# A Mamba-2 layer with a LoRA-expert branch on one Trainium2 core: VectorE turns every chunk's y, and B together with x, in the paired groups

## The reference

```python
xn = layernorm(x)                                  # x: 2048 tokens x 1024
proj = xn @ in_proj_w.T                            # gate 4096 | x 4096 | B 1024 | C 1024 | dt 64
x, B, C = split(silu(causal_conv4(proj_hbc)))      # 64 heads of 64; 8 groups, B and C 128 wide each
dt = softplus(dt + dt_bias); dA = exp(-exp(A_log) * dt)
state_t = state_{t-1} * dA_t + (dt_t * x_t) outer B_t ;  y_t = state_t @ C_t + x_t * D
yn = rmsnorm_by_group(y) * norm_weight * silu(gate)
out = x_in + yn @ out_proj_w.T + (xn @ W_base.T + b_base + top-2 LoRA experts)
```

## Time and profile before

| what | value |
|---|---|
| median of 3 runs | 3145.19 us (3144.51 to 3145.26) |
| the profiled execution, its own time | 3145.09 us |
| its span, first to last instruction | 3143.4 us |
| PE busy | 3126.1 us, 99% |
| DVE busy | 2558.5 us, 81% |
| ACT busy | 1704.5 us, 54% |
| POOL busy | 835.5 us, 27% |
| granted TensorE clock | 1.00 of full speed throughout |

### The profile page before, as it was taken

One profiled execution on the slowest core, in us unless ns is written; L12 is line 12 of the kernel. 1 busy time (PEld: TensorE's weight loads), 2 busy tenths in 40 slices (PEclk: granted clock), 3 DMA queues, 4 the chain that ended last, 5 costly groups with the idle time before them and its releaser, 6 DMA issues.

```text
span 3143.4 us, 55218 instructions
## 1 busy us (share of the span) xinstructions
PE 3126.1 (99%) x17660; PEld 2573.4 (82%) x17660; DVE 2558.5 (81%) x4599; ACT 1704.5 (54%) x4467; POOL 835.5 (27%) x917
## 2 busy tenths in 40 slices
PE   8999999999999999999999999999999999999999
PEld 7788888887888888888788888888878888888887
DVE  7977777785589999999648999999954988989983
ACT  5766666664265555656226555556533655565551
POOL 4444434433022222222103222222210222222220
PEclk9999999999999999999999999999999999999999
DMA  8777777777665555555566555555546555555554
GB/s 290 274 265 272 264 276 266 261 256 263 232 216 194 189 201 187 189 194 201 173 225 205 191 191 191 201 184 190 209 166 236 196 195 187 195 194 201 186 189 161
DMA packets 185668, 672.63 MB, mean 214 GB/s; under 512 B 21056, under 2 KB 22208, under 8 KB 185408
## 3 DMA queue, kind: packets, MB, share of 16 engines
q1 hardware_dynamic: 161280, 584.91, 53.3%
q10 hardware_dynamic: 24128, 84.42, 7.6%
...
## 4 chain that ended last, share of the span: by engine, by line
PE 95%; DVE 2%; ACT 1%; DMA 1%; issue 0%; SPq 0%; POOL 0%; ACTq 0%; DVEq 0%; POOLq 0%
PE dense L1072 21%; PE dense L1074 21%; PE dense L1073 21%; PE pX L1072 7%; PE pX L1074 7%; PE pX L1073 6%; PE pY L1187 3%; PE pD L1217 1%; PE pD L1187 1%; DVE conv_us L1497 1%; PE pCB L1163 1%; PE pU L1072 1%; PE pS L1073 1%; PE pS L1072 1%; PE pS L1074 1%; PE pU L1074 1%
## 5 line engine op out<-in xcount | busy, mean ns | idle before, releaser
L1072 PE MATMUL dense<-xn_hi,w_hl 128*128 128x512 f32 (+2 forms) x2192 | 869.7, 397 | 0.8 <-POOL w_hl L444 0.5
L1074 PE MATMUL dense<-xn_hi,w_hl 128*128 128x512 f32 (+2 forms) x2192 | 853.7, 389 | 0.0
L1073 PE MATMUL dense<-xn_lo,w_hl 128*128 128x512 f32 (+2 forms) x2192 | 852.0, 389 | 0.0
L1497 DVE SCALAR_TENSOR_TENSOR conv_us<-conv_in,const_g,conv_us 128x512 f32<-128x512 f32 x576 | 480.3, 834 | 47.0 <-ACT conv_us L694 33.2
L1074 PEld LDWEIGHTS dense<-xn_hi,w_hl 128*128 128x128 f32 (+1 forms) x2192 | 409.5, 187 | 88.9
L1072 PEld LDWEIGHTS dense<-xn_hi,w_hl 128*128 128x128 f32 (+1 forms) x2192 | 409.9, 187 | 86.0 <-issue 2.2
L1073 PEld LDWEIGHTS dense<-xn_lo,w_hl 128*128 128x128 f32 (+1 forms) x2192 | 410.3, 187 | 83.5 <-issue 1.2
L1072 PE MATMUL dense<-z_hi,w_hl 128*128 128x512 f32 x820 | 324.4, 396 | 1.6 <-DVE acc L1680 1.1
L501 POOL TENSOR_TENSOR C_lo<-BC,C_hi 128x128 fp32r<-128x128 f32 x120 | 60.0, 500 | 983.5 <-ACT S_hi L736 982.9
L1074 PE MATMUL dense<-z_hi,w_hl 128*128 128x512 f32 x820 | 319.7, 390 | 0.0
L1073 PE MATMUL dense<-z_lo,w_hl 128*128 128x512 f32 x820 | 319.1, 389 | 0.0
...
## 6 DMA issues: line engine op xcount, KB each, us to landing
...
cum_b<-cum_scratch ACTq DMA_DIRECT2D x128, 512.0 KB, 4.9
...
```

Source lines behind the costliest of these rows:

```text
L1072: nc.tensor.matmul(out, lhs[0], rhs[0], start=start, stop=False)
L1073: nc.tensor.matmul(out, lhs[0], rhs[1], start=False, stop=False)
L1074: return nc.tensor.matmul(out, lhs[1], rhs[0], start=False, stop=stop)
L1497: nc.vector.scalar_tensor_tensor(out=conv_u[r], in0=conv_in[r][:, t:t + TB], scalar=const_g[p][:, 4 * j + t:4 * j + t + 1], in1=conv_u[r], ...
```

## The change

All of it is in the paired groups (and what they call). It puts x and B into one tensor xBC, and `x_rows` turns x and B of two chunks together, as 16 transposes of 32x320 (5 tiles x 2 chunks x 32 tokens); `B_rows` goes. `yn_rows`, `gated_pair` and `gated_lo_pair` take chunks 2 and 3 as well, so `chunk_3` stays in a paired group for group 0's chunk 3 alone. On TensorE `chunk_1(0)` moves behind gate unit 2, and `chunk_2s(0)` and `chunk_2b(0)` behind out unit 0. ScalarE's `chunk_1` is split into `b_high`, `cs_high`, `ramps`, `wx_high` and `next_cum`, VectorE's into `wx_product`, `dtx_product`, `b_low` and `cb_masked`, and these are put into a new order. On VectorE x unit 2 goes ahead of y of chunks 2 and 3, x unit 3 behind it; turning y is spread between taps of tiles 4 and 5; silu of tile 3 comes ahead of tile 4's taps; silu of tile 5, the low part of z and `prep` move into the next group, behind the first quarter of `x_rows`. `chunk_2y` also waits for both products with dt.

```diff
 xn_lo = sb("xn_lo", [128, KD, TB], F32R)
 w_raw = [sb(f"w_raw{i}", [128, 1024]) for i in range(2)]
 w_hl = [sb(f"w_hl{i}", [128, 2, 2, 512], F32R) for i in range(2)]
-xT = [sb(f"xT{i}", [128, XT, TB]) for i in range(2)]
-BC = [sb(f"BC{i}", [128, 2, TB]) for i in range(2)]
+xBC = [sb(f"xBC{i}", [128, XT + 2, TB]) for i in range(2)]
+xT = [t[:, 0:XT, :] for t in xBC]
+BC = [t[:, XT:XT + 2, :] for t in xBC]
 BT, CT = ([bc[:, i, :] for bc in BC] for i in range(2))
 gate = sb("gate", [128, XT, TB])
 conv_us = sb("conv_us", [128, 2, TB])
...
-x_tm = sb("x_tm", [128, 2, GC])
-B_tm = sb("B_tm", [128, NC, N])
+x_tm = sb("x_tm", [128, 2, GC + N])
...
+    if not second:
+        normalize(0, 3)
     gate_unit(1)
-    chunk_1(g, p, 0, last, two=True)
-    z_high(g - 1, 3)
+    cs_high(g, p, 0)
+    if not second:
+        b_high(g, 0, True)
+        wx_high(g, 0)
+        z_high(0, 3)
+    gate_unit(2)
+    ramps(g, 0, True)
+    next_cum(g, 0, last)
+    gate_unit(3)
+    if second:
+        b_high(g, 0, True)
+        wx_high(g, 0)
     skip(g, 0)
-    gate_unit(2)
-    gate_unit(3)
     skip(g, 1)
-    chunk_1(g, p, 1, last, two=True)
+    b_high(g, 1, True)
+    wx_high(g, 1)
+    cs_high(g, p, 1)
+    ramps(g, 1, True)
+    next_cum(g, 1, last)
     if last:
         router_copy()
     mean_square(g, 0, True)
     mean_square(g, 1, True)
-    def normalize_pair():
-        normalize(g, 0, True)
-        normalize(g, 1, True)
-    chunk_1(g, p, 2, last, two=True, behind_wx=normalize_pair)
+    b_high(g, 2, True)
+    cs_high(g, p, 2)
+    wx_high(g, 2)
+    normalize(g, 0, True)
+    normalize(g, 1, True)
+    ramps(g, 2, True)
+    next_cum(g, 2, last)
     skip(g, 2)
     if not last:
         x_unit(0)
         ev_conv(g, K_X + 1, 1, turn_bank(12 + 1), p)
         tanh_conv(g, 0)
-    chunk_1(g, p, 3, last, two=True)
+    b_high(g, 3, True)
+    cs_high(g, p, 3)
+    wx_high(g, 3)
+    ramps(g, 3, True)
+    next_cum(g, 3, last)
     skip(g, 3)
-    z_high_pair(g, p)
+    z_high_pair(g, p, 0)
     if not last:
         x_unit(2)
         x_unit(3)
-        x_unit(4)
     mean_square(g, 2, True)
     mean_square(g, 3, True)
+    normalize(g, 2, True)
+    normalize(g, 3, True)
     if last:
-        normalize(7, 2, True)
-        normalize(7, 3, True)
-        z_high(7, 2)
-        z_high(7, 3)
+        z_high_pair(7, 1, 2)
     else:
-        normalize(g, 2, True)
-        x_unit(5)
-        z_high(g, 2)
+        x_unit(4)
+        ev_conv(g, K_X + 5, 5, turn_bank(12 + 5), p)
+        tanh_conv(g, 4)
+        z_high_pair(g, p, 2)
         tanh_conv(g, 5)
...
     gate_unit(g, False, 0, True)
-    if second:
-        chunk_3(g - 1, 2, two=True)
     gate_unit(g, False, 1, True)
+    gate_unit(g, False, 2, True)
+    if not second:
+        chunk_3(0, 3)
     chunk_1(g, 0, p, True, True)
-    gate_unit(g, False, 2, True)
-    chunk_3(g - 1, 3, two=second)
     gate_unit(g, False, 3, True)
+    out_units(g, 0, two=True)
     chunk_2s(g, 0)
     chunk_2b(g, 0)
-    out_units(g, 0, two=True)
+    out_units(g, 1, two=True)
     chunk_1(g, 1, p, True, True)
-    out_units(g, 1, two=True)
     if last:
         router_transpose()
     out_units(g, 2, two=True)
     chunk_2b(g, 3)
     chunk_2y(g, 2, True)
     chunk_2y(g, 3, True)
-    x_units(2)
-    if last:
-        chunk_3(7, 2, two=True)
-        x_units(1)
-        chunk_3(7, 3, two=True)
-        x_units(1)
+    x_units(4 if last else 2)
 group(0, 0, first=True)
...
     if first == 0:
-        dve.wait_ge(post, post_n(q, g, XT - 1))
+        dve.wait_ge(post, post_n(q, g, XT))
         dve.wait_ge(xd_done, chunk(q, g, c) + 1)
         dve.wait_ge(xw_done, chunk(q, g, c) * 2)
+        dve.wait_ge(ck_evac, chunk(q, g, c))
+        dve.wait_ge(bl_done, chunk(q, g, c))
     for f in range(first, end):
         for k in range(4):
-            src = xT[p][32 * f:32 * f + 32, :, :].rearrange("n j (c t) -> n j c t", c=NC)
-            dst = x_tm[32 * k:32 * k + 32, :, :].rearrange("p c (j i) -> p j c i", j=XT)
+            src = xBC[p][32 * f:32 * f + 32, 0:XT + 1, :].rearrange("n j (c t) -> n j c t", c=NC)
+            dst = x_tm[32 * k:32 * k + 32, :, :].rearrange("p c (j i) -> p j c i", j=XT + 1)
             ins = nc.vector.transpose(dst[:, :, :, 32 * f:32 * f + 32], src[:, :, c:c + 2, 32 * k:32 * k + 32])
     if end == 4:
         ins.then_inc(xt_done, 1)
-def B_rows(g, p, first, end):
-    if first == 0:
-        dve.wait_ge(post, post_n(q, g, XT))
-        dve.wait_ge(ck_evac, chunk(q, g, 0))
-        dve.wait_ge(bl_done, chunk(q, g, 0))
-    for f in range(first, end):
-        for k in range(4):
-            src = BT[p][32 * f:32 * f + 32, :].rearrange("n (c t) -> n c t", c=NC)[:, :, 32 * k:32 * k + 32]
-            ins = nc.vector.transpose(B_tm[32 * k:32 * k + 32, :, 32 * f:32 * f + 32], src)
...
+def wx_product(g, c):
+    if last_block and c == NC - 1:
+        return
+    if c == 0:
+        dve.wait_ge(prep_done, q * PREPS + g + 2)
+    dve.wait_ge(xt_done, xt_n(q, g, c))
+    nc.vector.tensor_tensor(heads(wx[:]), heads(x_tm[:, c % 2, 0:GC]), per_head(1, c), ALU.mult).then_inc(xw_done, 1)
+def dtx_product(g, c):
+    dve.wait_ge(xt_done, xt_n(q, g, c))
+    nc.vector.tensor_tensor(heads(dtx_2[c % 2]), heads(x_tm[:, c % 2, 0:GC]), per_head(0, c), ALU.mult)\
+        .then_inc(xw_done, 2 if last_block and c == NC - 1 else 1)
+def b_low(g, c):
+    dve.wait_ge(ck_evac, chunk(q, g, c) + 1)
+    nc.vector.tensor_tensor(B_lo[:], x_tm[:, c % 2, GC:GC + N], B_hi[:].bitcast(F32), ALU.subtract)\
+        .then_inc(bl_done, 1)
+def cb_masked(g, c):
+    dve.wait_ge(s1, chunk(q, g, c) * 2 + 2)
+    nc.vector.tensor_tensor(CBm, pCB[:, N:N + Q], causal[:], ALU.mult).then_inc(cbm_done, 1)
...
+def gated_pair(g, p, c):
+    cs = slice(c * Q, (c + 2) * Q)
     dve.wait_ge(gate_done, grp(q, g) * XT + XT)
-    dve.wait_ge(yt_done, (q - 1) * (G - 1) + g)
-    z = xT[p][:, :, 0:2 * Q]
-    nc.vector.tensor_tensor(z, z, gate[:, :, 0:2 * Q], ALU.mult).then_inc(z_done, 2)
...
             silu(g, 5, 1 - p)
-        if not first_block:
-            B_rows(g + 1, 1 - p, 0, 4)
         prep(g + 1)
...
     j_first = 1 if last else 0
-    x_rows(g, 0, p, 1 if second else 0, 4)
-    chunk_1_x(g, 0, True)
-    gated(g - 1, 3)
-    chunk_1_cb(g, 0, True)
-    gated_lo(g - 1, 3)
-    gate_tile(g, 0, False)
-    gate_tile(g, 1, False)
+    x_rows(g, 0, p, 0, 1)
+    if second:
+        silu(g - 1, 5, p)
+        gated_lo_pair(g - 1, 1 - p, 2)
+        prep(g)
+        x_rows(g, 0, p, 1, 2)
+        gate_tile(g, 0, False)
+        gate_tile(g, 1, False)
+        x_rows(g, 0, p, 2, 4)
+        wx_product(g, 0)
+        dtx_product(g, 0)
+        gate_tile(g, 2, False)
+        b_low(g, 0)
+    else:
+        x_rows(g, 0, p, 1, 4)
+        wx_product(g, 0)
+        gated(0, 3)
+        b_low(g, 0)
+        gated_lo(0, 3)
+        gate_tile(g, 0, False)
+        gate_tile(g, 1, False)
+        dtx_product(g, 0)
+        gate_tile(g, 2, False)
+    cb_masked(g, 0)
     masked(g, 0, True)
-    gate_tile(g, 2, False)
+    gate_tile(g, 3, False)
+    dve.wait_ge(acc_loaded, (q + 1) * 64)
+    out_adds(g, 0, halves=(0,), two=True)
     if last:
         router_weights()
+    out_adds(g, 0, halves=(1,), two=True)
     y_state(g, 0, True)
     y_skip(g, 0, True)
-    gate_tile(g, 3, False)
     state(g, 0)
-    dve.wait_ge(acc_loaded, (q + 1) * 64)
-    chunk_1_x(g, 1, True)
-    out_adds(g, 0, halves=(0,), two=True)
+    wx_product(g, 1)
+    dtx_product(g, 1)
+    b_low(g, 1)
     x_rows(g, 2, p, 0, 1)
-    out_adds(g, 0, halves=(1,), two=True)
-    x_rows(g, 2, p, 1, 2)
     if not last:
         consts_next(g, p)
     out_adds(g, 1, halves=(0,), two=True)
-    chunk_1_cb(g, 1, True)
+    x_rows(g, 2, p, 1, 2)
+    cb_masked(g, 1)
+    out_adds(g, 1, halves=(1,), two=True)
     x_rows(g, 2, p, 2, 3)
-    out_adds(g, 1, halves=(1,), two=True)
     masked(g, 1, True)
+    out_adds(g, 2, halves=(0,), two=True)
     x_rows(g, 2, p, 3, 4)
-    out_adds(g, 2, halves=(0,), two=True)
+    out_adds(g, 2, halves=(1,), two=True)
     y_state(g, 1, True)
-    out_adds(g, 2, halves=(1,), two=True)
     y_skip(g, 1, True)
     state(g, 1)
     y_intra(g, 0, True)
     y_intra(g, 1, True)
-    chunk_1_x(g, 2, True)
-    chunk_1_cb(g, 2, True)
+    wx_product(g, 2)
+    b_low(g, 2)
+    dtx_product(g, 2)
+    cb_masked(g, 2)
     out_adds(g, 3, halves=(0,), two=True)
-    yn_rows(g, p, 0, 1)
+    yn_rows(g, p, 0, 0, 1)
     out_adds(g, 3, halves=(1,), two=True)
-    yn_rows(g, p, 1, 3)
+    yn_rows(g, p, 0, 1, 3)
     if last:
         x_unit(0)
-    yn_rows(g, p, 3, 4)
+    yn_rows(g, p, 0, 3, 4)
     masked(g, 2, True)
     if last:
         x_unit(1)
     y_state(g, 2, True)
     y_skip(g, 2, True)
     state(g, 2)
-    gated_pair(g, p)
+    gated_pair(g, p, 0)
     if not last:
         x_unit(0)
-    chunk_1_x(g, 3, True)
+    wx_product(g, 3)
+    dtx_product(g, 3)
     x_unit(j_first + 1)
-    chunk_1_cb(g, 3, True)
```

(83 more changed lines are left out.)

109 lines of the change are left out of this document (68 added, 41 removed).

## The result

The changed kernel takes 3203.12 us (median of 4 runs, 3201.49 to 3204.52) against 3145.23 us (4 runs, 3144.51 to 3146.12): a ratio of 1.0184, 95% interval 1.0166 to 1.0201. The direction was forecast, the size was not: +58 us where the prediction had +19, and 3203 lies above the top of its range, 3182. The profiled execution took 3203.78, its span 3202.0.

What follows compares the result with a forecast made beforehand. TensorE was taken as the bound, VectorE nearly level; after the change VectorE would bound at 89.6 us a group against 87.1. At +6.4 a block, +19 in all, 3145.09 becomes 3164 us; whole range 3131 to 3182.

Steps and rivals of the forecast that it cites:

- TensorE's saving: On TensorE, each chunk_3 removed saves 0.48 us; 42 go in blocks 1 to 3, 20.2 us; a steady group needs 87.1.
- VectorE's sum: VectorE's need per steady group after the change: 87.5 + 7.1 - 5.0 + 2.2 - 0.1 - 3.3 + 1.2 = 89.6 us.
- the forecast distance: VectorE's x_tm transposes, grown from 256 to 320 columns, take about 0.51 us from start to start; +2.2 a group.
- The new wait: VectorE waits for normalised y before turning the second pair, behind x unit 3: +1.2 us a group, ends 0 and 1.7.
- The 1.55: VectorE's wait for conv_us before the taps of tile 3 goes, part of the -3.3 us a group.
- the waits of 1.27 that were to stay: VectorE's waits for the first pair's z_hi and y stay; 0 to -1.3 more if ScalarE's order removes one.
- The hold-up of gate tiles 0 and 1: Gate tiles wait for GpSimd's low part of S (1.29): VectorE needs 90.9, time 3184; rival with chance 0.10, left out of sum.
- B_lo of chunk 1: On VectorE before the change, it runs 0.80 for 0.28 while GpSimd makes wx_lo; with its end, taken as 0.6 us slack.
- the prediction's own formula: Per block, TensorE waits 5 x (89.6 - 87.1) + 0.6 = 13.1 and saves 14 x 0.48 = 6.7: +6.4 us.
- The prediction's "never" for a single SBUF input: VectorE instructions with one SBUF input are never locked out by GpSimd; those with two wait a whole instruction.
- the same meeting: TensorE's y product of chunk 3 meets VectorE's mask with 1.15 slack; 0.6 late in group 1, nothing added in group 7.
- The 0.6 of slack itself: Before the change VectorE by itself needs 88.07 - 0.6 = 87.5 us a group, against TensorE's 88.07.

Runs made afterwards that it cites:

- section 3: 15 of 16 transposes of the second pair's y left out: changed kernel 3153.16 us; two ScalarE moves added 3152.45; on section 4's 3135.38 us kernel 3124.88, 87.10 a group.
- r11_turn_late: Section 4's 3135.38 us kernel with the last 8 transposes of the first pair's y behind chunk 3's products, low z behind its mask: 3124.93 us.
- r2_gates: Changed kernel with ScalarE's high parts of C and S of chunk 0 moved behind gate unit 2 in groups 2 to 7: 3167.01 us, 89.6 a group.
- section 6: Rows of the kernel before; then the first pair's last 8 y transposes moved where GpSimd works, in reordered changed kernels: 3134.14, 3163.23 and 3124.93 us.
- sections 5 and 4: 5: kernel before with two wait-removing moves, 3144.97 us. 4: r2_gates with three such moves, 3135.38; also with high B and wx ahead of gate unit 3, 3155.32.

## Why the prediction was right and wrong

**TensorE's saving** was right: 0.48 for each of 42 `chunk_3`, 87.1 a group, shown by section 3 and, with all of the work done, by `r11_turn_late`.

**VectorE's sum** was right in its main terms. Four transposes of 32x320 take 2.05, 0.51 each; the forecast distance was 0.512. The new wait is 1.20 for 1.2. The 1.55 is gone. Smaller misses cancel: the waits of 1.27 that were to stay are 0.99 (z_hi) and 0.78 (yn), and a wait of 0.40 for B_hi has come. Without the two hold-ups the group is 89.6 (`r2_gates`), the very sum of the prediction, which to the tenth is luck, and 3167 is the forecast 3164 and 3 us.

**The step that failed** is "My sum leaves it out, since the two must coincide within a microsecond; its lower end is nothing." The hold-up of gate tiles 0 and 1 was costed, at most 1.3, and set aside with a chance of 0.10; it came in the steady groups, 1.0 each (all of them last the same 91.7 in blocks 1 and 2), under the decay of S right behind the low part that I had looked at. Coincidence was the wrong picture: what meets in one group meets in all 18, and GpSimd's two instructions cover 2.7 us, not one. The trace before had the evidence, which I did not read: taps and a silu held up by 1.0 and 0.85 in each of groups 1 to 6 of blocks 1 and 2 (section 6). The top of the range, 3182, even lay under my own 3184 for this rival. And I looked for such a meeting at one place only. B_lo of chunk 0 has the same form as B_lo of chunk 1, whose 0.80 for 0.28 I had read as slack; the change put it 1.8 us behind the wx product that starts GpSimd's wx_lo by way of ScalarE, and it stands 1.1. That has no term and no rival. With both, 89.6 + 2.1 = 91.7, as measured, and the prediction's own formula gives 5 x (91.7 - 87.1) + 0.6 - 6.7 = 16.9 a block, 51 us of the 58. The Trainium skill ("SBUF — State Buffer", section "SBUF: two separate sides") has a VectorE instruction with two SBUF inputs and a GpSimd one that reads SBUF hold each other off for a whole instruction, whichever starts first; the trace agrees here, with gate tiles, B_lo, silu and taps each 0.85 to 1.1 long under one. The prediction's "never" for a single SBUF input leaves out that the section excepts VectorE's 2-port modes; no experiment here was made on those.

**Two slips in the range.** By the prediction's own formula 90.5 a group gives 3178 and 91.0 gives 3185, not 3176 and 3184; neither brings in 3203.

**A second, smaller step**: "In group 7 TensorE has another unit ahead of the same meeting, so nothing is added." The waits of TensorE from group 7 to the end of group 1 of the next block:

```profile
PE pD L1225 <- DVE w_raw L1621: 1.5, 2, 1.0
PE pX L1110 <- DVE acc L1720: 0.8, 1, 0.8
PE pU L1308 <- DVE S_cur L1670: 0.7, 1, 0.7
```

Before, this stretch has no wait. Only one of the two waits at the y product, that of group 1, was in the sum (0.6; it is 1.0). The others come in group 7, at the adds, at the state that the router's transposes wait for, and at the mask of chunk 1; that VectorE enters this group late is my reading. From group 7 to the next group 2 the kernel takes 2.3 us more than before (171.0 + 69.5 + 98.4 against 172.5 + 74.5 + 89.6), where the formula has 0.6 and four `chunk_3` saved, -1.3. The waits are 3.0 and the saving 1.9; the other 1.2 stays open. In block 3 the formula errs the other way, since a group there took 87.4 and takes 90.6. The difference of the spans, 3202.0 - 3143.4 = 58.6, is thus 5 x (3.6 + 3.6 + 3.2) = 52 in the steady groups and some 7 outside them.

**Slack.** That waits of VectorE cost nothing before and nearly all of their length after is shown by sections 5 and 4. The 0.6 of slack itself no run measures; a sum built on it came out. What the prediction had as one bound, a sum per group, is two: experiment 3 shows that a stretch between two meetings with TensorE can be too long though the whole group has time to spare.
